# Second layer's query norms: 32 columns of ones on four column strips, factors on the turned scores, scores directly behind the sums

## The reference

```python
def _rmsnorm(x, w):
    xf = x.astype(jnp.float32)
    var = jnp.mean(xf * xf, axis=-1, keepdims=True)
    return (xf * jax.lax.rsqrt(var + EPS)).astype(x.dtype) * w
q = (hidden_states @ Wq.T).reshape(bsz, q_len, H, HD).transpose(0, 2, 1, 3)
k = (cross_attention_states @ Wk.T).reshape(bsz, kv_len, KVH, HD).transpose(0, 2, 1, 3)
...
q = _rmsnorm(q, q_norm_w)
k = jnp.repeat(k, GROUPS, axis=1)
...
k = _rmsnorm(k, k_norm_w)
scores = jnp.einsum('bhqd,bhkd->bhqk', q, k) * scale
scores = scores + attention_mask[:, :, :, :kv_len]
probs = jax.nn.softmax(scores.astype(jnp.float32), axis=-1).astype(q.dtype)
out = jnp.einsum('bhqk,bhkd->bhqd', probs, v)
```

## Time and profile before

| | us |
|---|---|
| median of 3 runs | 1300.31 (1298.08 to 1300.64) |
| profiled execution, span | 1297.6 |
| PE busy | 1227.0 (95%) |
| DVE busy | 792.7 (61%) |
| POOL busy | 576.0 (44%) |
| ACT busy | 493.4 (38%) |

### The profile page before, as it was taken

The page is one execution under the profiler, slowest core; times in us unless marked ns, Lnnn a source line. Parts: engine busy times, 40 slices in busy tenths (PEclk is TensorE's granted clock), DMA queues, the critical chain, the costliest instruction groups (busy, mean ns, idle before and its releaser), DMA issues.

```text
span 1297.6 us, 17051 instructions
## 1 busy us (share of the span) xinstructions
PE 1227.0 (95%) x6288; PEld 974.0 (75%) x6288; DVE 792.7 (61%) x1402; ACT 493.4 (38%) x763; POOL 576.0 (44%) x394
## 2 busy tenths in 40 slices
PE   7999999799999999998889999799999999999886
PEld 6887878587777777876678887577777777777665
DVE  4656645988888888888832243655444445544586
ACT  5144141222322222223441125555455565556522
POOL 4431432656756767664242111335444554544400
PEclk9999999899999999999899999899999999999987
DMA  7852830812122212112010003212122121211001
GB/s 259 267 158 102 259 114 24 309 41 81 65 81 73 73 52 102 41 41 97 1 57 33 1 0 127 82 41 74 41 73 73 48 72 73 73 41 41 33 1 65
DMA packets 57249, 106.74 MB, mean 82 GB/s; under 512 B 3504, under 2 KB 36272, under 8 KB 51824
## 3 DMA queue, kind: packets, MB, share of 16 engines
q1 hardware_dynamic: 56672, 105.04, 23.5%
q0 software_dynamic: 384, 1.05, 0.2%
q10 hardware_dynamic: 144, 0.00, 0.0%
HBM read 78.81 MB, written 27.26 MB: 82 GB/s over the span
## 4 chain that ended last, share of the span: by engine, by line
PE 71%; DVE 9%; POOL 7%; issue 6%; ACT 4%; DMA 1%; SPq 1%; POOLq 0%; ACTq 0%; DVEq 0%
PE ps_b L214 11%; PE ps_b L215 11%; PE ps_b L216 11%; PE ps_q L214 10%; PE ps_q L215 9%; PE ps_q L216 9%; PE ps_s L851 3%; PE ps_b L872 2%; PE ps_s L837 2%; POOL qT L1068 2%; POOL wo_lo L1061 2%; POOL wq_lo L681 1%; PE ps_s L256 1%; DVE o_lo L1214 1%; ACT wo_hi L955 1%
## 5 line engine op out<-in xcount | busy, mean ns | idle before, releaser
L214 PE MATMUL ps_b<-wo_hi,o_hi 128*128 128x512 f32 x512 | 203.9, 398 | 12.7 <-POOL wo_lo L1061 10.2
L214 PE MATMUL ps_q<-hT_hi,wq_hi 128*128 128x512 f32 x512 | 209.6, 409 | 2.1 <-ACT qT L963 2.1
L215 PE MATMUL ps_b<-wo_lo,o_hi 128*128 128x512 f32 x512 | 202.1, 395 | 0.0
L216 PE MATMUL ps_b<-wo_hi,o_lo 128*128 128x512 f32 x512 | 201.4, 393 | 0.0
L215 PE MATMUL ps_q<-hT_lo,wq_hi 128*128 128x512 f32 x512 | 200.9, 392 | 0.0
L216 PE MATMUL ps_q<-hT_hi,wq_lo 128*128 128x512 f32 x512 | 199.7, 390 | 0.0
L1068 POOL TENSOR_TENSOR qT<-q_t 128x512 f32<-128x512 f32 x64 | 89.8, 1403 | 92.0 <-DVE q_t L1156 92.0
L214 PEld LDWEIGHTS ps_q<-hT_hi,wq_hi 128*128 128x128 f32 x512 | 96.5, 189 | 43.7 <-issue 15.2
L1214 DVE TENSOR_TENSOR o_lo<-ps_b,o_hi 128x512 fp32r<-128x512 f32 x128 | 82.2, 684 | 73.9 <-ACT o_hi L988 73.4
L1223 DVE SCALAR_TENSOR_TENSOR x_sb<-ps_b,gates,x_sb 128x512 f32<-128x512 f32 x128 | 92.4, 726 | 55.0 <-PE ps_b L216 54.4
L214 PEld LDWEIGHTS ps_b<-wo_hi,o_hi 128*128 128x128 f32 x512 | 97.7, 191 | 36.8 <-issue 13.7
...
## 6 DMA issues: line engine op xcount, KB each, us to landing
...
```

The lines of the kernel that those rows point to most:

```text
L214: nc.tensor.matmul(dst, l_hi, r_hi, start=first, stop=False)
L215: nc.tensor.matmul(dst, l_hi, r_lo, start=False, stop=False)
L216: return nc.tensor.matmul(dst, l_lo, r_hi, start=False, stop=last)
```

## The change

The weights of the sums are 32 columns of ones instead of 64. The squares are taken in four parts (two sequences' halves each), each part as one matmul of 512 columns whose result lies on 32 partitions of its own; four such strips fill one bank, that of `ps_q` which is free at that time (`sums_bank`), and the banks of the projections alternate by `h` too (`query_bank`). DVE turns the bank in blocks of 32x32 (`turn_sums`), and eight copies of 32x16 bring one sum per query to the partition of its turned scores: `r_s`, 128x32. ACT's Ln and Exp run on these 32 columns. The scores come directly behind the sums, before the first projection, and wait for `s_turned` of the unit before instead of `r_ln`. DVE turns the scores from PSUM and then multiplies them in SBUF by the factors (`scale_scores`). The mask waits for `s_scaled`. The second projection waits until DVE has turned the sums.

```diff
--- before.py
+++ after.py
@@ -158,9 +158,10 @@
                 ("wo_raw", [P, J, E], F32))
-            pT, p_hi, p_lo, v_hi, v_lo, r_q, s_sb, p_sb = alloc(
+            pT, p_hi, p_lo, v_hi, v_lo, r_t, r_s, r_q, r_pad, s_sb, p_sb = alloc(
                 here, ("pT", [P, SC], F32), ("p_hi", [P, SC], FR), ("p_lo", [P, SC], FR), ("v_hi", [P, NT, D], FR), ("v_lo", [P, NT, D], FR),
-                ("r_q", [P, SC], F32), ("s_sb", [P, SC], F32), ("p_sb", [P, SC], F32))
+                ("r_t", [P, SC // 2], F32), ("r_s", [P, NQ], F32),
+                ("r_q", [P, NQ], F32), ("r_pad", [P, SC // 2 - 2 * NQ], F32), ("s_sb", [P, SC], F32), ("p_sb", [P, SC], F32))
             kT, qT = alloc(here, ("kT", [P, 2, HALF], F32), ("qT", [P, 2, J, HALF], F32))
...
@@ -707,7 +708,7 @@
             else:
-                eng.wait_ge(*c("s_turned", u + 1))
+                eng.wait_ge(*c("s_scaled", u + 1))
                 sc = s_sb.rearrange("p (n k) -> p n k", k=S)
...
@@ -808,43 +809,54 @@
+        def query_bank(lay, h, j):
+            return ps_q[(h + 1 + j) % 2 if lay else j % 2]
+        def sums_bank(h):
+            return ps_q[(h + 1) % 2]
         def att_pe(pe, lay, beside):
...
             def project(g, h, j):
-                n = 4 * (2 * g + h) + j
+                u = 2 * g + h
+                n = 4 * u + j
                 if h == 0:
...
                     pe.wait_ge(*c("wq_lo", 4 * g + j + 1))
-                if not (isinstance(g, int) and n < 2):
-                    pe.wait_ge(*c("q_rot" if lay else "q_read", n - 1))
+                if lay == 0:
+                    if not (isinstance(g, int) and n < 2):
+                        pe.wait_ge(*c("q_read", n - 1))
+                elif j == 1:
+                    if not (isinstance(g, int) and u == 0):
+                        pe.wait_ge(*c("ssq_t", u))
+                elif not (isinstance(g, int) and n == 0):
+                    pe.wait_ge(*c("q_rot", n if j == 0 else n - 1))
+                bank = query_bank(lay, h, j)
                 for k in range(KC):
-                    last = three(ps_q[j % 2][:, :], wq_hi[:, k, j * D:(j + 1) * D], wq_lo[:, k, j * D:(j + 1) * D],
+                    last = three(bank[:, :], wq_hi[:, k, j * D:(j + 1) * D], wq_lo[:, k, j * D:(j + 1) * D],
                                  hT_hi[:, k, h * HALF:(h + 1) * HALF], hT_lo[:, k, h * HALF:(h + 1) * HALF], k == 0, k == KC - 1)
...
             def square_sums(u, h):
                 pe.wait_ge(*c("q_sq", 4 * u + 4))
-                if isinstance(u, int) and u == 0:
-                    pe.wait_ge(*lns[2]("lo", NT))
-                else:
-                    pe.wait_ge(*c("s_scaled", u))
-                for t in range(PAIRS):
-                    for par in range(2):
-                        b = (2 * t + par) * S
-                        last = nc.tensor.matmul(ps_s[par * S:(par + 1) * S, t * JS:(t + 1) * JS], ones[:, :], q_sq[:, :, b:b + S],
-                                                start=True, stop=True)
+                pe.wait_ge(*c("q_rot", 4 * u + 3))
+                squares = q_sq.rearrange("p j (t c q) -> p c t j q", t=PAIRS, c=4)
+                for k in range(4):
+                    last = nc.tensor.matmul(sums_bank(h)[k * QB:(k + 1) * QB, :], ones[:, 0:QB], squares[:, k], start=True, stop=True)
                 last.then_inc(c["ssq"], 1)
             def score(u, h, g):
...
                 pe.wait_ge(*c(f"k_in{h}", 16 * (g + 1)))
-                if lay:
-                    pe.wait_ge(*c("r_ln", u + 1))
-                elif not (isinstance(u, int) and u == 0):
+                if not (isinstance(u, int) and u == 0):
                     pe.wait_ge(*c("s_turned", u))
+                elif lay:
+                    pe.wait_ge(*lns[2]("lo", NT))
                 for t in range(PAIRS):
...
@@ -894,14 +906,16 @@
                     return
-                if do_score and lay and not (isinstance(g, int) and (g, h) == (1, 0)):
-                    square_sums(us, 1 - h)
+                if do_score and lay:
+                    if not (isinstance(g, int) and (g, h) == (1, 0)):
+                        square_sums(us, 1 - h)
+                    score(us, 1 - h, g if h else g - 1)
                 at_first = lay and isinstance(g, int) and (g, h) == (0, 0)
...
                     project(g, h, 1)
-                if do_score:
+                if do_score and lay == 0:
                     score(us, 1 - h, g if h else g - 1)
...
@@ -959,15 +973,16 @@
                     act.wait_ge(*c("ssq", u))
-                nc.scalar.activation(q_sq[:, j, :], ps_q[j % 2][:, :], ACT.Square).then_inc(c["q_sq"], 1)
-                nc.scalar.activation(qT[:, h, j, :], ps_q[j % 2][:, :], ACT.Copy, scale=qk_w[:, 0:1]).then_inc(c["q_rot"], 1)
+                bank = query_bank(lay, h, j)
+                nc.scalar.activation(q_sq[:, j, :], bank[:, :], ACT.Square).then_inc(c["q_sq"], 1)
+                nc.scalar.activation(qT[:, h, j, :], bank[:, :], ACT.Copy, scale=qk_w[:, 0:1]).then_inc(c["q_rot"], 1)
             def norms(u):
-                act.wait_ge(*c("ssq", u + 1))
+                act.wait_ge(*c("ssq_all", u + 1))
                 if not (isinstance(u, int) and u == 0):
                     act.wait_ge(*c("s_scaled", u))
-                nc.scalar.activation(r_q[:, :], ps_s[:, :], ACT.Ln, bias=eps_rms[:, 0:1]).then_inc(c["r_ln"], 1)
+                nc.scalar.activation(r_q[:, :], r_s[:, :], ACT.Ln, bias=eps_rms[:, 0:1]).then_inc(c["r_ln"], 1)
                 act.wait_ge(*c("r_ln", u + 1))
...
@@ -1155,27 +1170,34 @@
-            def scale_scores(u):
+            def turn_scores(u, h):
                 dve.wait_ge(*c("scored", u + 1))
-                dve.wait_ge(*c("r_q", u + 1))
-                if isinstance(u, int) and u == 2 * G - 1:
-                    dve.wait_ge(*c("p_turned", u))
-                nc.vector.tensor_tensor(p_sb[:, :], ps_s[:, :], r_q[:, :], ALU.mult).then_inc(c["s_scaled"], 1)
-            def turn_scores(u, h):
-                src = ps_s[:, :]
-                if lay == 0:
-                    dve.wait_ge(*c("scored", u + 1))
-                else:
-                    if not (isinstance(u, int) and u == 2 * G - 1):
-                        scale_scores(u)
-                    dve.wait_ge(*c("s_scaled", u + 1))
-                    src = p_sb[:, :]
-                nc.vector.transpose(s_sb[:, :], src).then_inc(c["s_turned"], 1)
+                nc.vector.transpose(s_sb[:, :], ps_s[:, :]).then_inc(c["s_turned"], 1)
                 if lay == 0:
                     att_mask(dve, lay, u, h)
+            def turn_sums(u, h):
+                dve.wait_ge(*c("ssq", u + 1))
+                nc.vector.transpose(r_t[:, :], sums_bank(h)[:, :]).then_inc(c["ssq_t"], 1)
+                dve.wait_ge(*c("ssq_t", u + 1))
+                if not (isinstance(u, int) and u == 0):
+                    dve.wait_ge(*c("r_ln", u))
+                sums_of = r_t.rearrange("p (n q) -> p n q", q=QB)
+                for k in range(4):
+                    for qh in range(2):
+                        src = 2 * (k // 2) + qh
+                        last = nc.vector.tensor_copy(r_s.rearrange("p (n a) -> p n a", a=2)[k * QB:(k + 1) * QB, :, qh],
+                                                     sums_of[src * QB:(src + 1) * QB, :, 0])
+                last.then_inc(c["ssq_all"], 1)
+            def scale_scores(u):
+                dve.wait_ge(*c("r_q", u + 1))
+                dve.wait_ge(*c("s_turned", u + 1))
+                sc = s_sb.rearrange("p (n k) -> p n k", k=QB)
+                nc.vector.tensor_tensor(sc, sc, wide(r_q[:, :], QB), ALU.mult).then_inc(c["s_scaled"], 1)
             def across(dst, src):
@@ -1251,7 +1273,9 @@
                 if second_first_scores(lay, g, h):
+                    turn_sums(us, 1 - h)
                     turn_scores(us, 1 - h)
+                    scale_scores(us)
                     dve.wait_ge(*c("mask_in", 16))
...
@@ -1275,7 +1299,11 @@
                 if do_score:
+                    if lay:
+                        turn_sums(us, 1 - h)
                     turn_scores(us, 1 - h)
+                    if lay:
+                        scale_scores(us)
                 rotated(1)
...
@@ -1310,8 +1338,10 @@
             else:
+                turn_sums(last, 1)
+            turn_scores(last, 1)
+            if lay:
                 scale_scores(last)
-            turn_scores(last, 1)
             out_low(last - 1, 0)
...
```

## The result

The changed kernel takes 1304.89 us, the median of 12 runs (1301.34 to 1309.22), beside 1300.20 for the kernel before in 12 runs of the same comparison (1298.08 to 1303.65). The ratio is 1.0041, 95% interval 1.0030 to 1.0052: slower by some 4.7 us. The forecast was 1302.8, in a range of 1292 to 1311. The profiled execution has a span of 1302.1 us beside 1297.6.

The account below looks back on a forecast made before the run. PE, busy 95% of the span, was taken as the bound. Terms -7.4 + 4.0 + 0 - 0.9 - 2.2 + 5.6 + 3.4 = +2.5 us on the 1300.31 median gave 1302.8 us, range 1292 to 1311.

Parts of the forecast that it names:

- seven steps with h = 1: Steps (1,1) to (7,1), bound by PE: sums and scores save 1.05 us each, -7.4 us in all.
- h = 0 loop steps, later `qT`: Five loop steps: ACT waits for DVE's copies, held by POOL, so `qT` comes 0.8 us later each; +4.0 us.
- clock: Five h = 0 loop steps: PE idles about 2.3 us, two fall to 1.2 GHz at 1.7 us each; +3.4 us.
- step (7,0): Outside the loop: table loaded ahead of the wait spares 1.28 us, copies late alike; 0.
- last sums and end: Unit 15's sums save 0.9 us; its norms, waiting for DVE, delay `p_hi` of unit 14 and what follows, +5.6.
- start: Start of the layer: earlier DVE chain to the exponentials 1.5 us, PE's shorter wait 0.7; together -2.2 us.
- rival (1): Sums on PE: only two strips run at a time, sums stay at 1.88 us; +9.3, 1309.6 us; chance 0.20.
- (2): Sums on PE: matmuls start in strict order, five rounds instead of two, 2.35 us; 1315.4 us; chance 0.03.
- Rival (3): DVE's copies aren't held by POOL; h = 0 steps gain 0.1 us each, clock stays up; -6.3, 1294.0; chance 0.14.
- rival (4): End of the layer: delay hidden because something else there was about to be as late; 1297.2 us; chance 0.08.
- The second part: Start of the layer: PE's 2.22 us wait before the scores vanishes, later projections wait instead; 0.7 us left as gain.

Follow-up runs that it names:

- the table of four: h = 1 step lengths: kernel before 27.80 us, strips alone 26.93, position of the scores alone 27.43, both (changed kernel) 26.72.

## Why the prediction was right, point by point

**The sum.** +2.5 us was forecast and +4.5 measured in the profiled execution (+4.7 by the medians), the right sign, and each wait stood where it was said. By its terms:

| term | forecast | measured |
|---|---|---|
| seven steps with h = 1 | -7.4 | -7.56 |
| h = 0 loop steps, later `qT` | +4.0 | +3.4 (0.66 and 0.70 in the two at full clock) |
| clock | +3.4 (two falls of 1.7) | +4.9 (three falls of 1.6) |
| step (7,0) | 0 | +0.10 |
| last sums and end | -0.9 + 5.6 = +4.7 | +4.79 |
| start | -2.2 | -1.12 |

The sign rests on the clock term, which was a guess. Without it the forecast is -0.9 and the measured change -0.4 us: the gain on PE and the new waits cancel, and what makes the kernel slower by more than the 0.2% that a measurement can tell is the falls of the clock. One profiled execution shows three of them; how many there were in the other eleven runs isn't known. So the waits were foreseen, but that they came out as slower was luck. The errors of the terms, -0.2, -0.6, +1.5, +0.1, +0.1 and +1.1, cancel only in part.

**Sums on PE.** Two rounds on four strips, as taken: 0.99 us to the scores, and 1.08 saved per step for 1.05 forecast. Rivals (1) and (2) fall with the row of 938.12: it leaves room neither for four rounds nor for five. The time alone would not have told rival (1) from the forecast: its price was 1309.6, but the sums with 64 columns, which take its 1.88 us, measured 1304.52, since the shorter wait of PE keeps the clock up. Rival (1) left the clock term as it was. The Trainium skill (TensorEngine Tiling, Key Properties) says that a change of tiling mode drains the engine. The trace agrees in so far as such passages take time, and the table of four gives a price: both parts together save 1.08 where the two alone sum to 1.24. The 0.16 us between them I put down to the passage from 32 to 64 columns, which of these four only the changed kernel has; no run isolates it. The split was near as well: 0.94 for the strips and 0.1 for the passage were forecast, 0.87 and 0.21 measured.

The Trainium skill (TensorE: Matmul & The Clock Gate, Part 3) gives 2.38 times for three strips, by which, as an estimate, a step would have saved some 0.75 us. No such inefficiency shows here: 1.08.

**h = 0 steps.** Each link came as forecast: transposition 0.72, first copy ended by `p_lo`, load 4.4 us behind the start of the sums (4.38), PE's wait 2.19 (2.3 forecast). Rival (3) fell with the first copy's 1.05 us, and the copies from PSUM showed that POOL is its cause. They also bear out what rival (3) said of these steps: PE's wait is 1.36 us (1.4 said), the clock stays up, the loop's h = 0 steps are 0.11 us shorter than in the kernel before (0.1 said), and step (7,0) 0.8 (0.9 said).

**Clock.** The one term that was an even guess. It was put at two falls of five; there were three, and four in the run with the scores moved back. In the h = 0 steps the falls go by the length of the wait. In the loop's they stand behind none of ten waits of 1.36 to 1.49 us, ten of fifteen of 1.94 to 2.21 us, and all twelve of 3.55 to 3.79 us (five with the copies doubled, seven in the kernel before reordered, of which two in steps (1,0) and (7,0)). Elsewhere in (1,0) and (7,0), waits of 2.37, 2.96 and 3.03 us had a fall each and 2.22 us in the kernel before had none. The price, 1.6 us, was taken nearly right from the earlier trace rows (1.7). What decides between the ten and the five is open.

**The start** is the term that was mis-sized, by 1.1 us. The step that takes 1.5 of the 3 us by which DVE's chain to the exponentials could be earlier, the rest being held up by POOL until 821.3, was too hopeful: 0.45 came. I had counted the hold for the copies that were held before, not that all four would be. POOL is also busier here: its `wo_lo` and `wq_lo` beside DVE's scaling and mask took 1.75 and 2.26 us (1.29 each before), and it ran without a gap up to 820.85, where it had idled 1.27 us for ACT. The second part, -0.7, came as forecast: PE's wait of 2.22 us before the scores became one of 1.51 before the third projection, 0.71 less, and the sums of unit 2 follow those of unit 1 0.67 us sooner.

**The end** was right to 0.1 us in sum and in place, 4.79 for 4.7, and rival (4) fell with `p_hi` at 1227.33. What the prediction didn't see is how little a plain repair would bring there: it named only the first of three waits in a row.
